# A two-layer attention kernel: its setup in a new order, with other bias transfers and another sigmoid

## The reference

```python
h = silu(ln(pos @ w0 + b0, g0))     # (positions, 512)
h = silu(ln(h @ w1 + b1, g1))
h = h @ w2 + b2                     # (positions, 16 heads)
bias = h[i - j + n - 1]             # bias of head, query i, key j
```

## Time and profile before

| | |
|---|---|
| time, median of 3 runs | 2467.25 us (2465.68 to 2468.71) |
| the profiled execution: its time | 2467.19 us |
| the profiled execution: its span | 2465.4 us |
| TensorE busy | 2383.4 us, 97% |
| VectorE, ScalarE, GpSimd busy | 1642.0, 1631.4, 902.9 us |
| end of the setup (last low part) | about 78 us |
| first instruction of the main block on TensorE | 81.1 us |

### The profile page before, as it was taken

How to read it: one execution, slowest core, us unless ns; L and a number is a source line. 1 busy time by engine, 2 the same in 40 slices (tenths; PEclk the granted TensorE clock), 3 DMA queues, 4 the chain that set the end, 5 groups by cost and what they waited for, 6 DMA issues and landing times.

```text
span 2465.4 us, 53983 instructions
## 1 busy us (share of the span) xinstructions
PE 2383.4 (97%) x16801; PEld 2087.3 (85%) x16801; DVE 1642.0 (67%) x4685; ACT 1631.4 (66%) x6621; POOL 902.9 (37%) x1691
## 2 busy tenths in 40 slices
PE   1699999999999999999999999999999999999998
PEld 0588888888888888888888888888888888888887
DVE  5566766766766766766766766766766766766766
ACT  2466666666666666666666666666666666666665
POOL 0333433433433433433433433433433433433432
PEclk7799999999999999999999999999999999999999
DMA  6101101101101101101101101101101101101101
GB/s 200 40 29 46 41 28 45 41 28 45 41 28 45 41 28 45 41 28 45 41 28 45 41 28 45 41 28 45 41 28 45 41 28 45 41 28 45 41 24 36
DMA packets 94907, 102.24 MB, mean 41 GB/s; under 512 B 47616, under 2 KB 49696, under 8 KB 94880
## 3 DMA queue, kind: packets, MB, share of 16 engines
q1 hardware_dynamic: 90192, 99.90, 13.1%
q10 hardware_dynamic: 4688, 2.01, 0.4%
HBM read 48.89 MB, written 16.79 MB: 27 GB/s over the span
## 4 chain that ended last, share of the span: by engine, by line
PE 96%; DVE 0%; ACT 0%; issue 0%; POOL 0%; POOLq 0%; DVEq 0%
PE psum L351 33%; PE psum L431 29%; PE psum L417 10%; PE psum L385 10%; PE psum L397 6%; PE psum L368 5%; PE psum L338 3%; PE psum L359 1%; ACT probs L514 0%; DVE probs L631 0%; DVE neg_max L638 0%; DVE x_lo L582 0%; POOL weights L738 0%; ACT x_hi L473 0%; DVE x_out L666 0%
## 5 line engine op out<-in xcount | busy, mean ns | idle before, releaser
L738 POOL TENSOR_TENSOR weights<-probs,den_inv 128x256 f32<-128x256 f32 (+3 forms) x1024 | 466.3, 484 | 1468.7 <-DVE den_inv L644 1460.8
L514 ACT ACTIVATE probs<-probs,neg_max 128x129 f32<-128x129 f32 (+3 forms) x2048 | 717.2, 353 | 373.4 <-DVE neg_max L638 373.4
L725 POOL TENSOR_TENSOR masked_bias<-bias,pad_neg 128x516 f32<-128x516 f32 (+3 forms) x512 | 392.9, 800 | 15.3 <-POOL pad_neg L721 9.0
L631 DVE TENSOR_TENSOR probs<-psum,masked_bias 128x324 f32<-128x324 f32 x512 | 225.4, 482 | 257.8 <-PE psum L385 257.8
L514 ACT ACTIVATION_READ_ACCUMULATOR probs<-probs,neg_max 128x1 f32 x2048 | 387.0, 189 | 0.0
L351 PE MATMUL psum<-w_hi,x_hi 128*128 128x384 f32 x1536 | 337.9, 342 | 4.4 <-DVE x_lo L582 4.4
L351 PE MATMUL psum<-w_hi,x_lo 128*128 128x384 f32 x1536 | 330.3, 337 | 0.0
L351 PE MATMUL psum<-w_lo,x_hi 128*128 128x384 f32 x1536 | 329.9, 337 | 0.0
L351 PEld LDWEIGHTS psum<-w_hi,x_hi 128*128 128x128 f32 x1536 | 273.0, 190 | 16.7 <-DVE x_lo L582 5.3
L385 PEld LDWEIGHTS psum<-keys,q_t 64*128 64x128 f32 x4096 | 238.6, 188 | 49.4 <-issue 49.4
L351 PEld LDWEIGHTS psum<-w_lo,x_hi 128*128 128x128 f32 x1536 | 273.2, 189 | 0.0
(11 more groups left out here) (111 smaller groups left out, 3219.0 us busy)
## 6 DMA issues: line engine op xcount, KB each, us to landing
xa<-in_x_dram SPq DMA_DIRECT2D x64, 256.0 KB, 2.6
x_res<-in_x_dram SPq DMA_DIRECT2D x64, 256.0 KB, 2.6
out_dram<-x_out SPq DMA_DIRECT2D x64, 256.0 KB, 2.1
x_in<-x SPq DMA_DIRECT2D x62, 256.0 KB, 2.3
x_res<-x_in SPq DMA_DIRECT2D x62, 256.0 KB, 2.3
raw<-in_L_cond_Wq_dram SPq DMA_DIRECT2D x8, 512.0 KB, 7.5
raw<-in_L_cond_Wo_dram SPq DMA_DIRECT2D x8, 256.0 KB, 5.1
raw<-in_L_cond_Wout_dram SPq DMA_DIRECT2D x8, 256.0 KB, 7.2
```

Of the source, the lines that this page charges most:

```text
L514: x_ = nc.scalar.activation(s, s, ACT.Exp, bias=neg_max[:, g, k, e:e + 1], accum_out=den[:, g, k, e:e + 1])
L631: a = nc.vector.tensor_tensor(probs[:, 2 * c + e, :], SB[c][e][:, 0:ROW], masked_bias[u.layer][:, 2 * c + e, :], ALU.add)
L725: m = nc.gpsimd.tensor_tensor(block(masked_bias[u.layer], b), block(bias[u.layer], b), pad_neg[u.layer][:, 0:WIDTH[b]].unsqueeze(1).to_bro ...
L738: m = nc.gpsimd.tensor_tensor(places[b], block(pairs(probs, g // 2), b)[:, :, 1:1 + n], den_inv[:, g, k, :].unsqueeze(2).to_broadcast([P, ...
```

## The change

- The order of the pieces is "in" 0, "out" 0, "in" 1, "out" 1; every low part is made by VectorE; the two transfers of a `Wo` piece are one; `between` is new.
- ScalarE's first loads are the three rows of the first layer, then g_in, the other two rows, and eight loads of null biases (a strip of 32 partitions and four values each). SyncE's first are w1, w2, b2; the null loads follow at piece 4, the rest at piece 6.
- The null key's arithmetic moves from before the network to after its phases 7 and 9.
- The sigmoid is exp(-ln(1 + exp(-h))), three activations on ScalarE, with h cut off at -80.
- The L0 bias comes in 16 loads and the diagonals in 16, each of four heads (one per strip) over all 128 partitions; SyncE issues eight of the latter and ScalarE eight. The null biases are placed by 8 copies instead of 32.
- `v_part` is zeroed behind the first normalisation.

```diff
@@ main block, VectorE
             def begin(u):
                 run_stages((input_statistics, u), (normalise, u))
+                for n in range(2):
+                    nc.vector.memset(v_part[n][:, :, :], 0.0).then_inc(v_part_zeroed, 1)
+                dve.wait_ge(v_part_zeroed, 2)
...
-            for n in range(2):
-                nc.vector.memset(v_part[n][:, :, :], 0.0).then_inc(v_part_zeroed, 1)
-            dve.wait_ge(v_part_zeroed, 2)
@@ setup, loads
-        gain_loads += [(null_bias[n][:, :], row(L["null_bias"], H)) for n, L in enumerate(layers)]
+        for n, L in enumerate(layers):
+            for t, strip in enumerate(strips):
+                gain_loads += [(null_bias[n][strip, :], bass.AP(L["null_bias"].tensor, 2 * t, [[0, R], [8, 2], [1, 2]]))]
...
-        for t in range(4):
-            for c in range(2):
+        for c in range(2):
+            for e in range(2):
                 for b in range(BLOCKS):
-                    heads = bias0[8 * c + 2 * t:8 * c + 2 * t + 2, b * R:(b + 1) * R, 0:(b + 1) * R]
-                    rest_loads += [(block(bias[0][strips[t], 2 * c:2 * c + 2, :], b)[:, :, 1:], heads.rearrange("e q k -> q e k"))]
+                    heads = bias0[:, b * R:(b + 1) * R, 0:(b + 1) * R].rearrange("(c t e) q k -> c e t q k", c=2, e=2)[c, e]
+                    rest_loads += [(block(bias[0][:, 2 * c + e, :], b)[:, 1:], heads)]
...
-        pieces = [("in", n, c) for n in range(2) for c in range(KC)] + [("out", n, c) for n in range(2) for c in range(PAIRS // 2)]
-        IN = 2 * KC
-        lo_engine = ["pool" if kind == "out" and c % 2 else "dve" for kind, n, c in pieces[:-1]] + ["dve"]
+        pieces = [(kind, n, c) for n in range(2) for kind, count in (("in", KC), ("out", PAIRS // 2)) for c in range(count)]
...
-        between = [0, 0, 0, 0, 3, 1, 0, 1, 1, 0]
+        between = [0, 0, 0, 1, 3, 1, 1, 1, 1, 1]
...
+        def load_diagonals(eng, c):
+            eng.wait_ge(diag_stored, 32)
+            for e in range(2):
+                for b in range(BLOCKS):
+                    eng.dma_start(block(bias[1][:, 2 * c + e, :], b)[:, 1:],
+                                  bass.AP(diagonals.tensor, (8 * c + e) * 2 * S + (BLOCKS - 1 - b) * R,
+                                          [[4 * S, 4], [1, R], [1, R * (b + 1)]])).then_inc(diag_loaded[c], 16)
@@ setup, VectorE
                 def normed(layer):
-                    dve.wait_ge(act_step, 4 + 3 * layer)
-                    step(V.tensor_scalar(h[:, :], h[:, :], rs[:, 1:2], None, ALU.mult), f"normed {layer}")
+                    dve.wait_ge(act_step, 2 + 5 * layer)
+                    step(V.tensor_scalar(sig[:, :], h[:, :], rs[:, 1:2], -80.0, ALU.mult, ALU.max), f"normed {layer}")
+                    step(V.tensor_scalar(h[:, :], h[:, :], rs[:, 1:2], None, ALU.mult))
 
                 def silu(layer):
-                    dve.wait_ge(act_step, 5 + 3 * layer)
-                    step(V.tensor_scalar(sig[:, :], sig[:, :], 1.0, None, ALU.add))
-                    step(V.reciprocal(sig[:, :], sig[:, :]))
+                    dve.wait_ge(act_step, 5 + 5 * layer)
                     step(V.tensor_tensor(h[:, :], h[:, :], sig[:, :], ALU.mult), f"silu {layer}")
...
                 def place_null_biases():
                     dve.wait_ge(gain_loaded, 16 * len(gain_loads))
                     for n in range(2):
-                        for t, strip in enumerate(strips):
-                            for b in range(BLOCKS):
-                                V.tensor_copy(...).then_inc(null_placed, 1)
+                        for b in range(BLOCKS):
+                            V.tensor_copy(block(bias[n], b)[:, :, 0], null_bias[n][:, :]).then_inc(null_placed, 1)
...
                         if k == 3:
                             place_null_biases()
+                        if k == 7:
+                            null_key()
+                        if k == 9:
+                            null_key_scaled()
@@ setup, SyncE
-                start(sp, null_loads, null_loaded)
+                start(sp, w1_loads, w1_loaded)
                 for i, (kind, n, c) in enumerate(pieces):
-                    if i == 5:
-                        start(sp, w1_loads, w1_loaded)
-                    if i == IN:
+                    if i == KC:
+                        start(sp, null_loads, null_loaded)
+                    if i == KC + 2:
                         start(sp, rest_loads, rest_loaded)
...
                 for dst, src, loaded in first_loads:
                     sp.dma_start(dst, src).then_inc(loaded, 16)
+                load_diagonals(sp, 0)
@@ setup, ScalarE
-                start(act, gain_loads, gain_loaded)
-                start(act, rows_loads, rows_loaded)
+                start(act, rows_loads[:3], rows_loaded[0])
+                start(act, gain_loads[:2], gain_loaded)
+                start(act, rows_loads[3:], rows_loaded[1])
+                start(act, gain_loads[2:], gain_loaded)
...
-                    step(f"normed {layer}", lambda: nc.scalar.activation(sig[:, :], h[:, :], ACT.Exp, scale=-1.0))
+                    step(f"normed {layer}", lambda: nc.scalar.activation(sig[:, :], sig[:, :], ACT.Exp, scale=-1.0))
+                    step(f"normed {layer}", lambda: nc.scalar.activation(sig[:, :], sig[:, :], ACT.Ln, bias=1.0))
+                    step(f"normed {layer}", lambda: nc.scalar.activation(sig[:, :], sig[:, :], ACT.Exp, scale=-1.0))
...
-                    if k == sum(between) + 1:
-                        act.wait_ge(diag_stored, 32)
...
+                    if k == sum(between):
+                        load_diagonals(act, 1)
```

More of the change, by code:

```diff
@@ L768, in setup @@
         null_k_col = sb("null_k_col", [P, 1])
-        null_bias = [sb(f"null_bias{n}", [P, H]) for n in range(2)]
+        null_bias = [sb(f"null_bias{n}", [P, 4]) for n in range(2)]
         scale_col = sb("scale_col", [P, 2])
@@ L833, in wait_piece @@
         def wait_piece(eng, i):
-            eng.wait_ge(raw_loaded[i % RAW], 32 * (i // RAW + 1))
-        def wait_lo(eng, i):
-            eng.wait_ge(lo_done[lo_engine[i]], sum(e == lo_engine[i] for e in lo_engine[:i + 1]))
+            eng.wait_ge(raw_loaded[i % RAW], sum(32 if pieces[j][0] == "in" else 16 for j in range(i % RAW, i + 1, RAW)))
         order = []
-        between = [0, 0, 0, 0, 3, 1, 0, 1, 1, 0]
+        between = [0, 0, 0, 1, 3, 1, 1, 1, 1, 1]
         for phase, count in enumerate(between):
@@ L921, in _, with null_key, null_key_scaled @@
                 step(V.memset(k_scale[0][:, :], DH ** -0.5))
[L923 to L931, removed]
+                def null_key():
+                    dve.wait_ge(null_loaded, 16 * len(null_loads))
+                    step(V.tensor_tensor(nk_sq[:, :], null_k[:, :], null_k[:, :], ALU.mult))
+                    step(V.tensor_reduce(nk[:, 0:1], nk_sq[:, :], AX.X, ALU.add))
+                    step(V.tensor_scalar(nk[:, 1:2], nk[:, 0:1], NORM_FLOOR, None, ALU.max), "null key's norm")
+                    step(V.scalar_tensor_tensor(k_scale[1][:, :], scale_col[:, 0:1], 8.0, scale_col[:, 1:2], ALU.mult, ALU.mult))
+                    step(V.tensor_tensor(keys[0][:, 0:1], null_k_col[:, :], k_scale[0][:, :], ALU.mult))
+                def null_key_scaled():
+                    dve.wait_ge(act_step, 12)
+                    step(V.tensor_tensor(null_k_col[:, :], null_k_col[:, :], nk[:, 3:4], ALU.mult))
+                    step(V.tensor_tensor(keys[1][:, 0:1], null_k_col[:, :], k_scale[1][:, :], ALU.mult))
                 def place_null_biases():
@@ L965, in _ @@
                     else:
-                        for k in range(2):
-                            j = 2 * c + k
-                            sp.dma_start(raw[:, slot, k * D:(k + 1) * D], L["Wo"][j * P:(j + 1) * P, :]).then_inc(loaded, 16)
+                        sp.dma_start(raw[:, slot, 0:2 * D].rearrange("p (j d) -> p j d", j=2),
+                                     L["Wo"][2 * c * P:2 * (c + 1) * P, :].rearrange("(j p) d -> p j d", p=P)).then_inc(loaded, 16)
                 for dst, src, loaded in first_loads:
                     sp.dma_start(dst, src).then_inc(loaded, 16)
+                load_diagonals(sp, 0)
             @program.scalar
@@ L999, in rstd, with sigmoid, null_norm @@
                     step(f"statistics {layer}", lambda: nc.scalar.activation(rs[:, 1:2], rs[:, 0:1], ACT.Exp, scale=-0.5))
-                def exponential(layer):
-                    step(f"normed {layer}", lambda: nc.scalar.activation(sig[:, :], h[:, :], ACT.Exp, scale=-1.0))
+                def sigmoid(layer):
+                    step(f"normed {layer}", lambda: nc.scalar.activation(sig[:, :], sig[:, :], ACT.Exp, scale=-1.0))
+                    step(f"normed {layer}", lambda: nc.scalar.activation(sig[:, :], sig[:, :], ACT.Ln, bias=1.0))
+                    step(f"normed {layer}", lambda: nc.scalar.activation(sig[:, :], sig[:, :], ACT.Exp, scale=-1.0))
+                def null_norm():
```

(8 more changed lines are left out.)

38 lines of the change are left out of this document (12 added, 26 removed).

## The result

The changed kernel takes 2455.2 us (median; 2454.1 to 2456.7) against 2466.8 us before: ratio 0.9952, 95% interval 0.9940 to 0.9964. It is 11.5 us faster; I had forecast 25 us, a range of its own of 2436 to 2448, and with rivals 1 and 2 one that ended at 2453. The profiled execution took 2455.07 us (span 2453.2).

The account below looks back on a forecast made before the run. TensorE bounds the loop, left alone; the setup before it, one path of loads, network, store, issues and last pieces, can shrink. 6.4 + 5.0 - 1.3 - 1.5 + 16.0 + 0.55 = 25.1 off 2467.2 gives 2442 us, range 2436 to 2448.

Parts of the forecast that it names:

- Rival 1: New four-headed loads spread over only 4 of 16 DMA engines, 5.5 us more: 2448 us; chance 0.27.
- Rival 2: ScalarE's 15 issues cost 1.02 us each, so its queue holds the network 5.8 us: 2448 us; chance 0.08.
- C: Order on VectorE: copies and low parts before the second layer hidden beside matmuls; elsewhere 1.3 us more (0 to 2.5).
- E: Diagonals' store to setup end: 15.9 us instead of 31.9, so 16.0 us less.
- A: Head of the relative-bias network: starts 6.4 us earlier (5.8 to 7.4), no longer waiting for nine null loads.
- D: SyncE's queue: pieces 6 to 8 issued behind null and rest loads, 1.5 us more (0 to 5).
- B: Sigmoid as three activations: 2.15 us instead of 4.68, twice, 5.0 us less.
- nothing for: Parts credited with no gain or cost: fewer bias0 loads, merged `Wo` loads, the narrower null_bias.
- the tie: At the setup's end: flips and copy done at 53 at the latest, VectorE's low parts at 53.5, VectorE ending it.
- F: `v_part` memsets go behind the first normalisation, where VectorE waits anyway: 0.55 us less.
- Rival 3: Slower: four engines with dearer packets, above 46 ns each; at 55 ns 2477 us; chance 0.04.

Follow-up runs that it names:

- f4: The changed kernel with the old sigmoid (one exponential on ScalarE, add and reciprocal on VectorE); 2455.8 us.
- e2: The changed kernel, but the first high part waits for the two g_in loads alone and null biases are placed after the network's last phase; 2456.9 us.
- h2: The changed kernel with the old null biases: two row broadcasts and 32 copies instead of eight strip loads and 8 copies; 2453.2 us.
- e3: The changed kernel with both edits of e1 and e2: diagonal loads with 32 rows outermost, null biases placed after the network; 2452.5 us.
- f1: e3 with SyncE's queue reordered: pieces 4 to 6 behind piece 3, null loads behind piece 8, null key's arithmetic behind the network; 2449.5 us.
- e4: The kernel before with four-headed loads alone: 16 instead of 32 for input bias and for diagonals, the latter all on ScalarE; 2464.8 us.
- h1: g2 without GpSimd's queue: SyncE issues eight input bias loads between pieces 6 and 7, eight behind its diagonal loads; 2446.2 us.
- e1: The changed kernel with its 16 diagonal loads having 32 rows outermost instead of four heads; 2452.7 us.
- g1: The changed kernel with the 16 input bias loads issued by GpSimd instead of SyncE; 2470.4 us.
- g2: e3 with f1's queue order, the 16 input bias loads on GpSimd's queue, and ScalarE's diagonal loads one high part later; 2467.0 us.

## Why the prediction was wrong

Most mechanisms were the right ones. The steps that failed are C (a wait that I had at nothing: "hidden"), E (the store's landing at 2.1 us, eight issues at 4.8, and which chain ends last), and A in size; D failed too, but C hid it. 12.8 us are missing at the main block (66.59 against 53.8).

- **A, head of the network.** Said 6.4, measured 14.89 - 10.32 = 4.6. The third row, issued at 1.80, ended the wait at 10.3: 8.4 us, where I had taken 6.5 (medians by kind 6.0 to 9.6, and 5.5 to 7.1 before). The likely reason, argued and not tested, is that w1 and the first pieces, moved to the front of SyncE's queue, run beside them (DMA share 1.08 in 7 to 17 us); I had taken landings from a stretch where that queue carried only nine small loads. (w1 stood in that queue's twentieth place, not its eleventh; nothing hangs on it.) Missing: 1.8. Rival 2, ScalarE's queue, was near: its issues end at 11.4 and the first activation came at 12.06 when its input was ready.
- **B, sigmoid.** Each as said (2.14 us, said 2.15). Its length was right, and f4 shows that in the end only 1.1 of the 5.0 counted: the first saving went into the wait for the null biases, most of the second into the way of the diagonals behind the store.
- **C, order on VectorE.** "5.5 us beside 6.12 us of matmuls: hidden." This is the step that failed first. I counted the copies and not the loads that they wait for: `place_null_biases` waits for all ten gain loads, eight of them new, issued last on ScalarE's queue. It cost 29.08 - 23.35 = 5.7, less 1.0 for matmuls that ran faster than before (5.09 instead of 6.12; the same eight took 5.1 to 6.8 us from run to run, so this 1.0 is luck): 4.7 missing. e2 and h2 show the cause. The narrower null_bias, which I had put under "nothing for", is most of it: with the old loads (h2) the second layer stands 1.9 us behind its matmuls, not 5.7.
- **D, SyncE's queue.** Said: piece 8 issued by 27.7. Measured: piece 6 at 33.8. The range for the queue's stops was right to be there, and the row of b2 was the right warning. In this kernel the step didn't cost more than said, which was luck: since C had made everybody else late, ScalarE waited only 2.77 us for piece 6, and the part from the second layer to the store took 14.0 instead of 14.9, 0.9 less than said. With C mended (e3 against f1) the step costs the store 6.0 us, four times the 1.5 and outside its bounds of 0 to 5.
- **E, store to end.** Said 15.9, measured 66.30 - 43.12 = 23.2, of which: store to first load 5.96 instead of 2.1 (+3.9; the stores landed in 4.8 and 5.6 us, while pieces filled the DMA engines, share 1.05 in 43 to 48.7 us, and in 1.6 in the kernel before with a share of 0.20; e4 had 4.6 at 0.98, and f1, where pieces were not in the way at first, 1.7 and 3.4 at 0.46); eight issues 7.22 instead of 4.8 (+2.4); high and low parts 8.6 instead of 9.0 (-0.4); and the flips and copies end it, not VectorE (+1.4). The chain that ended it reads: first load 49.08, landed 61.41 (12.3 us), flips and copies to 66.30 (4.9). I had 2.9 for the last two, for two groups of flips; both queues land together now, so all four groups come behind. And my own bounds did not give the tie: 51.5 + 2.5 + 0.4 is 54.4, not "53 at the latest". The store's landing before:

```profile
diagonals<-diag_t ACTq DMA_DIRECT2D x1, 8.0 KB, 1.6
```
- **F** and the low parts as said: the memsets stand beside the transposes, a `Wo` low part takes 1.2.

1.8 + 4.7 - 0.9 + 7.3 = 12.9. h1, with C and D mended and the diagonals spread, has the store at 36.91 (said 37.6), the first load 5.8 us later (said 2.1), and ends 13.7 us after that (said 13.8, though GpSimd's additions end it and not VectorE): the store's landing is what is left.

Rival 1 was a part of it. The profile showed it (share flat at 0.30, 5 semaphore updates a load), e1 and e3 measured it at 2.2 and 4.3 us, less than the 5.5 that I had given it. The rule behind it in the Trainium skill ("DMA: Bandwidth & Descriptors", "Why a DMA increments its semaphore by 16 and not by 1") agrees with the trace: with four heads outermost a load raised its semaphore 4 times as its data landed, with 32 rows 16 times. I had given it 0.27 and held against it that nothing in the trace showed such a spreading, but the trace had no load of this shape, so it said nothing either way. Rival 3 asked for 46 ns a packet; 16 loads of 128 packets from 49.1 to 61.4 on four engines are 12.3 x 4 / 2048 = 24 ns at most, since the first 3 us were shared with pieces; from 52 to 60 us, at 76 GB/s and a mean row of 320 B, it is about 17 (my estimate from these rows). So it was far.

## What to carry to other kernels

Count for every moved wait the loads behind it, and price a load by the stretch it will land in, not by the one it comes from: the same `rows` went from 7.1 to 9.5 us, a small store from 1.6 to 5.6. When two waits lie side by side, mending either shows nothing (e2: 4.2 us gained at the second layer, none at the store; g1: pieces in time, none at the store); mend both before judging one. Put a long dimension outermost on both sides of a load (32 rows instead of four heads took the eight issues from 8.4 to 4.8 us, e2 against e3), and look for a flat share in the table of stretches.

## What the runs showed of the hardware that I had not expected

- An issue on SyncE's queue can stand for microseconds: two `g_out` issues took 5.88 us in the changed kernel (6.80 in e2) and 0.43 each before. They stand soon after nine small null loads, but those are not all of it: with the null loads behind them (f1) the two took 1.76, and the `null_v` load just before them 2.85 (2.08 in the changed kernel). The cause is open.
- The eight strip loads of the null biases, 0.5 KB each, landed 10.2 us after their issues, later than 0.5 MB pieces (medians 7.4 to 9.7).
- GpSimd's queue stood idle for 1.9 to 7 us between two of these loads (g2), where SyncE took 0.65 to 1.25 us a load, issue and all.
- The same eight matmuls of the second layer took 5.1 to 6.8 us from run to run.
